# Mixture of experts by dispatch: each row through its two experts only, in place of every row through all eight

## The reference

```python
scores = xf @ gate_w.T                       # 8 experts
ew, ei = jax.lax.top_k(scores, 2)
ew = jax.nn.softmax(ew, axis=-1)
x1 = jax.nn.silu(jnp.einsum('td,ehd->teh', xf, w_gate))      # 128 hidden features per expert
x3 = jnp.einsum('td,ehd->teh', xf, w_up)
expert_out = jnp.einsum('teh,edh->ted', x1 * x3, w_down)
comb = jnp.einsum('ta,tae->te', ew, jax.nn.one_hot(ei, 8))
routed = jnp.einsum('te,ted->td', comb, expert_out)
shared = jax.nn.silu(xf @ sh_gate.T) * (xf @ sh_up.T) @ sh_down.T    # 256 hidden features
return routed + jax.nn.sigmoid(xf @ se_gate_w.T) * shared
```

## Time and profile before

| | us |
|---|---|
| median of 3 runs | 524.58 (524.57 to 527.5) |
| span of the profiled execution, first to last instruction | 524.4 |
| TensorE busy | 485.8 (93%), 3744 matmuls |
| VectorE busy | 383.4 (73%) |
| ScalarE busy | 217.7 (42%) |
| GpSimd busy | 155.0 (30%) |
| mean granted clock of TensorE, as a share of 2.4 GHz | 0.978 |

### The profile page before, as it was taken

One profiled execution on the slowest core, in us unless ns is written; L12 is line 12 of the kernel. 1 busy time (PEld: TensorE's weight loads), 2 busy tenths in 40 slices (PEclk: granted clock), 3 DMA queues, 4 the chain that ended last, 5 costly groups with the idle time before them and its releaser, 6 DMA issues. The chain is left out here.

```text
span 524.4 us, 11913 instructions
## 1 busy us (share of the span) xinstructions
PE 485.8 (93%) x3744; PEld 426.8 (81%) x3744; DVE 383.4 (73%) x1159; ACT 217.7 (42%) x501; POOL 155.0 (30%) x287
## 2 busy tenths in 40 slices
PE   3789999998999999999999999998899889699996
PEld 2567777776888888888888888887888878699995
DVE  5578777777777777777777776788788698666542
ACT  4444555542333333333333335553555444454540
POOL 3434444432111111111111121246455465632100
PEclk9999999999999999999999999998999799899999
DMA  8522222111000000000000000000000000000111
GB/s 279 166 57 62 58 58 58 38 41 45 16 17 16 15 15 15 15 15 15 15 15 15 16 11 11 21 22 22 12 19 20 10 1 2 0 22 22 40 40 42
DMA packets 15088, 18.06 MB, mean 34 GB/s; under 512 B 2001, under 2 KB 14546, under 8 KB 15058
## 3 DMA queue, kind: packets, MB, share of 16 engines
q1 hardware_dynamic: 15058, 17.69, 11.3%
HBM read 15.59 MB, written 2.10 MB: 34 GB/s over the span
## 5 line engine op out<-in xcount | busy, mean ns | idle before, releaser
L251 PE MATMUL PS<-wfh,arena_r 128*128 128x256 f32 (+2 forms) x352 | 121.3, 345 | 1.4 <-DVE arena_r L855 1.4
L252 PE MATMUL PS<-wfl,arena_r 128*128 128x256 f32 (+2 forms) x352 | 116.1, 330 | 0.0
L253 PE MATMUL PS<-wfh,arena_r 128*128 128x256 f32 (+2 forms) x352 | 116.1, 330 | 0.0
L276 POOL TENSOR_TENSOR ve<-mv,eps 128x1 f32<-128x1 f32 x64 | 12.8, 201 | 221.3 <-DVE mv L270 221.0
L251 PEld LDWEIGHTS PS<-wfh,arena_r 128*128 128x128 f32 x352 | 66.6, 189 | 10.1 <-DVE arena_r L855 4.8
L253 PEld LDWEIGHTS PS<-wfh,arena_r 128*128 128x128 f32 x352 | 66.6, 189 | 7.2
L252 PEld LDWEIGHTS PS<-wfl,arena_r 128*128 128x128 f32 x352 | 66.6, 189 | 4.9
L592 ACT ACTIVATE arena_r<-PS 128x512 fp32r<-128x512 f32 (+1 forms) x48 | 25.1, 526 | 62.2 <-PE PS L1187 62.2
L597 ACT ACTIVATE arena_f<-PS 128x512 f32<-128x512 f32 (+1 forms) x48 | 25.3, 527 | 53.0 <-PE PS L253 52.8
L286 DVE TENSOR_SCALAR arena_f<-x,mv,rstd 128x256 f32 (+1 forms) x48 | 37.0, 771 | 13.7 <-POOL rstd L279 13.3
L874 DVE SCALAR_TENSOR_TENSOR arena_f<-arena_f,tiny,PS 128x128 f32<-128x128 f32 x144 | 43.2, 356 | 0.6
(11 more groups left out here) (137 smaller groups left out, 1245.2 us busy)
## 6 DMA issues: line engine op xcount, KB each, us to landing
ctx_raw<-in_ctxT SPq DMA_DIRECT2D x32, 128.0 KB, 2.1
raw<-in_w_ffn SPq DMA_DIRECT2D x16, 241.0 KB, 2.6
raw<-in_w_l SPq DMA_DIRECT2D x16, 192.0 KB, 2.4
out<-arena_f SPq DMA_DIRECT2D x8, 256.0 KB, 2.2
x<-in_x SPq DMA_DIRECT2D x1, 1792.0 KB, 9.9
raw<-in_w_l SPq DMA_DIRECT2D x2, 512.0 KB, 5.0
rows<-in_rows SPq DMA_DIRECT2D x1, 640.0 KB, 6.1
x<-in_x SPq DMA_DIRECT2D x1, 256.0 KB, 2.8
```

Source lines behind the costliest of these rows:

```text
L251: nc.tensor.matmul(out_ap, lh, rh, start=first, stop=False)
L252: nc.tensor.matmul(out_ap, lh, rl, start=False, stop=False)
L253: return nc.tensor.matmul(out_ap, ll, rh, start=False, stop=last)
```

## The change

The router goes into stage 0, and the experts run after it on rows sorted by expert.

- **Stage 0** (`each_slot`: all slots written out, no loop; so too on VectorE and GpSimd in stage 2): in slot `s` tile `s - 3`, whose `x` is complete, is normalised (`route_stats` on VectorE; `route_rstd`, three small operations on GpSimd; `route_norm` on ScalarE), transposed (`route_T`) and split (`route_hi`, `route_lo`) into `xT2h`, `xT2l`, which hold all 2048 tokens by feature in the space of the layer-1 weights. `route`, in slot `s` for tile `s - 4`, makes the scores; VectorE's `route_top` takes the maximum and its index. The last tiles' steps lie in stage 1.
- **Shared expert**: four groups of 512 tokens, two slices of 128 hidden features each, feature-major, so without transposes of the hidden features: `shared_in` (six matmuls of 512, for gate and for up), tanh, two VectorE passes, high and low half, and `shared_out` per tile (six matmuls of 256). `add_shared` adds it to `x` with the sigmoid gate as factor.
- **Places**: `choose` marks each token's two experts; two small plain float32 products (`count_members`, `rank_members`) give each token its rank within its expert; `places` makes its row number, expert `e` having a region of 2176 rows in the DRAM tensor `xs_rows`.
- **Scatter**: `keep_rows` (ScalarE) writes all normalised tiles to `xs`; GpSimd issues two indirect DMAs per tile, 32 in all, each of 128 rows of 1 KB. Block tails are zeroed by SyncE (9 DMAs). `block_table` and `result_places` compute, on VectorE, which expert and rows each of the 40 blocks has and where each result will lie.
- **Blocks**: 40 blocks of 128 rows, in 20 pairs. SyncE reads two row numbers into registers and loads two blocks (128 KB each), four pairs ahead; TensorE transposes them (`block_T`), reads one register word per pair that gives the weight columns, and does `block_in` (per block six matmuls of 256: gate and up of one expert), `block_hT` and `block_down` (three matmuls of 256 per block). ScalarE and VectorE do the halves and the silu. SyncE stores each pair (256 KB) to `ys_rows`. The layer-1 weights are loaded and split beside the blocks.
- **Gather**: after the last store GpSimd gathers for each tile the two result rows of each token (two indirect DMAs), tiles 0 to 2 ahead of stage 2, tile `s + 3` in slot `s` of it; VectorE's `combine` adds them to `x` with their weights (two passes) ahead of the normalisation.

The diff, cut to its core:

```diff
+REGION = TOKENS + P
+BLOCKS, TAIL = 40, 8
+BPAIRS = BLOCKS // 2
...
+            sp.wait_ge(R["tails"], 2)
+            for e in range(EXPERTS):
+                row = sp.value_load(tail_i[0:1, e:e + 1], min_val=0, max_val=XROWS - P)
+                load(xs_d[bass.ds(row, P), :], zeros, tails_zeroed)
+            sp.wait_ge(R["rows"], 1)
...
+            sp.wait_ge(tails_zeroed, 16 * (EXPERTS + 1))
+            sp.wait_ge(rows_scattered, 16 * 2 * TILES)
+            for j in range(4):
+                load_block(j)
+            for j in range(BPAIRS):
+                if j + 4 < BPAIRS:
+                    load_block(j + 4)
+                if j < TILES:
+                    load_w(1, j, j % 2)
+                if j >= 1:
+                    store_block(j - 1)
+            store_block(BPAIRS - 1)
...
+            pool.wait_ge(R["place"], 4)
+            for t in range(TILES):
+                pool.wait_ge(S1["xs"], t + 1)
+                for k in range(2):
+                    nc.gpsimd.indirect_dma_start(
+                        out=xs_d, out_offset=bass.IndirectOffsetOnAxis(posi[:, k, t:t + 1], 0), in_=xs[:, t, :],
+                        in_offset=None).then_inc(rows_scattered, 16)
...
+            def gather(t):
+                if t >= 2:
+                    pool.wait_ge(x_done[1], t - 1)
+                for k in range(2):
+                    nc.gpsimd.indirect_dma_start(
+                        out=gy[:, t % 2, k, :], out_offset=None, in_=ys_d,
+                        in_offset=bass.IndirectOffsetOnAxis(posy[:, k, t:t + 1], 0)).then_inc(y_row_in[t % 2], 16)
+            pool.wait_ge(w_lo, 2 * TILES)
+            pool.wait_ge(R["first"], 6)
+            for r in range(2):
+                pool.wait_ge(y_stored[r], 16 * BPAIRS // 2)
+            for t in range(2):
+                gather(t)
+            for t in range(2):
+                ln_rstd_step(pool, 2, t, t)
+            gather(2)
+            ln_rstd_step(pool, 2, 2, 0)
...
+            for t in range(2):
+                combine(t)
+                ln_stats_step(dve, 2, t, t)
+                ln_aggr_step(dve, 2, t, t)
+            for t in range(2):
+                ln_norm_step(dve, 2, t, t, xn)
+            combine(2)
+            ln_stats_step(dve, 2, 2, 0)
+            ln_aggr_step(dve, 2, 2, 0)
+            for t in range(2):
+                xT_lo_step(dve, 2, t, t, X_T)
+            ln_norm_step(dve, 2, 2, 0, xn)
...
+            for j in range(BPAIRS + 1):
+                if j < BPAIRS:
+                    word = pe.value_load(word_i[0:1, j:j + 1], min_val=0, max_val=(1 << 22) - 1)
+                    gate_at = [pe.snap((word >> 4) & 0x780), pe.snap(word & 0x780)]
+                    down_at[j] = [pe.snap((word >> 11) & 0x700), pe.snap((word >> 7) & 0x700)]
+                    block_in(j, 0, gate_at[0])
+                if j >= 1:
+                    block_hT(j - 1)
+                if j < BPAIRS:
+                    block_in(j, 1, gate_at[1])
+                if j + 2 < BPAIRS:
+                    block_T(j + 2)
+                if j >= 1:
+                    block_down(j - 1, down_at.pop(j - 1))
...
+            pe.wait_ge(w_lo, 2 * TILES)
+            pair_keys(0)
+            for t in range(2):
+                transpose_x(pe, 2, t, t, X_T)
+            pair_queries(0)
```

More of the change, by code:

```diff
@@ L25 @@
 ACT = mybir.ActivationFunctionType
+AXIS = mybir.AxisListType
 P = 128
@@ L109, in slots, with each_slot @@
         body(Slot(s, s % 2, count))
+def each_slot(first, last, body):
+    for s in range(first, last + 1):
+        body(Slot(s, s % 2, TILES))
 def after(eng, sem, t, back=0, base=0, per=1, extra=0):
@@ L373, in build @@
             "o_psum")}
+        R = {n: sem("route_" + n) for n in (
+            "setup", "below", "weights_hi", "weights", "moments", "shift", "xn", "T", "hi", "lo", "psum", "scores", "top",
+            "gap", "gap_e", "mix", "member", "count_psum", "counts", "place", "table", "rows", "words", "tails", "first")}
         S1 = {n: sem("s1_" + n) for n in (
-            "router_psum", "scores", "top", "index", "gap", "gap_exp", "denom", "weights", "w2", "indexf", "pick1",
-            "pick2", "comb", "g_psum", "u_psum", "tanh", "a", "h", "hT_psum", "hT_hi", "hT_lo", "down")}
+            "g_psum", "u_psum", "tanh", "a", "h", "h_hi", "h_lo", "o_psum", "xs")}
+        E = {n: sem("e_" + n) for n in (
+            "T", "x_hi", "x_lo", "gu", "tanh", "a", "h", "hT", "h_hi", "h_lo", "y", "y_out")}
+        x_shared = sem("x_shared")
         S2 = {n: sem("s2_" + n) for n in (
@@ L991, in slot2 @@
                 here, before, leaving, ahead = s.tile(0), s.tile(-1), s.tile(-2), normalised_in(s)
+                if ahead and s.tile(2):
+                    combine(ahead[0])
                 if ahead:
```

819 lines of the change are left out of this document (577 added, 242 removed).

## The result

The changed kernel takes 573.85 us (median of 4 runs, 572.38 to 579.96) against 524.58 before: a ratio of 1.094 (95% interval 1.088 to 1.101), slower where 505 had been forecast. The span of its profiled execution is 571.2, so 46.8 us more than before.

A forecast was written before the change was run, and what follows sets the result against it. TensorE was taken to bound stage 0 and the dense experts, no single engine stage 2. 524.4 + 13.6 (stage 0) - 56 (first shared product to stage 2's queries) + 19 (stage 2) + 4 (clock) = 505 us; range 472 to 540.

The forecast's parts named there:

- Step 1: Stage 0: the router adds 1.0 us a tile on TensorE, +13 over 13 tiles, plus 0.6 before the first shared product.
- Step 2: Shared expert, 512 tokens at a time: the engines are through 42 us after the first shared product (T0').
- Step 3: Scatter: row numbers 16 us after the first shared product (T0'), 32 issues 38.4, then 7.6 to the first expert product.
- X: Price of one indirect DMA issue on GpSimd, taken as 1.2 us; the forecast's range was 0.8 to 1.6.
- Step 4: Expert blocks: 40 blocks in 20 pairs at 3.3 us a pair, 66 us (54 to 90).
- rival (d): Expert blocks run at 4.5 us a pair, by landing times or register reads: +24, 529 in all; chance 0.07.
- Step 5: From blocks to stage 2's queries (Tq'): last output 3.2 us, then 16 with the queries waiting for the third gather.
- Step 6: Stage 2 with gathers: 1.2 us more a tile (0.85 for VectorE's passes, 0.35 more), +19 (0 to +40).
- step 7: TensorE's clock at 1.2 instead of 2.4 GHz: 2 us after each of two stands, +4 (0 to +15).
- (b): Scatter and gathers: the list of indirect DMAs sets both ends; at X = 2.5, 573 us in all; chance 0.16.
- (a): Scatter and gathers: indirect DMA issues are cheap, X = 0.45, 477 us in all; chance 0.20.
- (c): Stage 2: VectorE and GpSimd block each other, a tile costs 10 instead of 7.6, +38, 524 in all; chance 0.07.

The follow-up runs named there:

- the variant of the late transpose: Changed kernel with router statistics one slot earlier, and the router's transpose behind the gate product, its eviction behind the gate's tanh: 539.20 us (ratio 1.022).
- the variant with early statistics: Changed kernel with the router's row statistics taken by VectorE one slot earlier, right behind the addition completing the tile: 552.05 us (ratio 1.052).
- section 6: Row numbers of tiles 0 to 7 made in stage 0, against reordered router, single weight offset, earlier query halves, 2560 descriptor bytes: 530.75 us (ratio 1.007).

## Why the prediction was wrong, point by point

By spans 571.2 against 505.0, 66.2 off: stage 0 +39.0, T0' to Tq' +33.9, the rest -6.8.

**Step 1, the router in stage 0: the step that failed.** The sum of TensorE's work was right (7.5 a tile once the chain is gone). What failed is the sentence "TensorE is the limit, so the work is not hidden: 13 x 1.0": it priced the added instructions and not the wait that came with them. The bound had been named, "a stall of an in-order engine at every tile", +26, and was dismissed without following who must be done before whom: statistics, three GpSimd steps, normalisation, transpose, all inside one slot. That stall, with the clock of 0.84 that it drew after it (1.00 in the same window once it was gone), made +52.7 in place of +13.6, twice the bound that was given. The experiments give back 31.0 of the 39.0. Of the other 8, two waits of 1.84 and 2.67 us are seen in the last two slots (at 133.79 and 138.72 in the variant of the late transpose), which have no gate or query products to hide the chain; the rest was not followed up.

**Step 2, shared expert at T0' + 42:** too short by some 7 us even where nothing stood still (TensorE through at +48.6 in the variant with early statistics), and by 32 here: VectorE's last addition ended at +74, beside the standing still, which no row of before had shown.

**Step 3, scatter.** Numbers at +16: 16.2. X = 1.2: 1.27. Scatter 38.4: 44.4, of which 3.6 are the two pauses of 2.11, beyond the usual gap of 0.30, which no step had; with 2560 bytes for descriptors there was one, of 2.16. The 7.6 to the first product: 17.0, since "The engines' 42 is covered by this" was false here (in the two other profiles of this kernel the first block came 6.4 sooner behind the last issue). For 128 rows an issue took 0.96 on GpSimd and 1.27 from issue to issue, the same for rows of 64 bytes and of a kilobyte. So in a series of 32 it is the issue on GpSimd that counts (44.4 in all); the landing comes once, within the 5.4 from the last issue's end to the first block where nothing stood still.

**Step 4, blocks at 3.3 a pair:** 4.05, 82 us in place of 66. The mis-sized term is "a register read, which no row prices, with some eight register steps of 0.03, 0.2 to 0.5 together": it measured 0.66 to 0.77 a pair, and there were 21 register steps, not eight, at distances of 0.10 or more, not 0.03. Without the register work the pairs come every 3.4 us, near the forecast's 3.3. That was rival (d)'s mechanism, at two thirds of its price; and "if pairs take over 4" was one of the signs of being wrong that the prediction had named.

**Step 5, results back 19.2:** 21.3 (333.2 to 354.45), by the steps told: the third gather sets the queries.

**Step 6, stage 2 at 8.8 a tile, +19, and step 7, clock +4:** step 7's 1.2 GHz is what the trace of before shows at a granted clock of 0.50 (363 to 367): products of 256 columns start 0.213 apart there, 1.2 columns a ns, and 0.12 apart after 369; its 2.4 is the double, for a clock of 1.00. The two steps are together 23, measured 16.2 (18.4 and 20.1 in the two other profiles). The additions took 0.61 and 0.57 a tile, more than the 0.85 counted; the gathers' 0.35 a tile was not there in the run with half of them.

**The rivals.** (b) gave 573 and the measurement is 573.85; it was still not what happened, for X is 1.27, below its point of decision of 1.6. Its number agrees by chance. (a) is out by X. (c): GpSimd's gathers in stage 2 took 0.997 us beside a busy VectorE and 0.979 in the scatter. So the issues show no blocking between the two. VectorE is stretched beside GpSimd's arithmetic, though: 7 of its 26 additions in that stage took 0.73 to 0.96 in place of 0.48, each of them beside GpSimd's own addition to `x` (L651), while its normalisations beside nothing but a gather's issue took 0.41, as alone.

## What to carry to other kernels

When work is moved into a pipelined slot, write down for each added instruction who must be done first, and check that the whole chain of small steps across engines starts a slot before its end is needed; its price is the wait, which the sum of busy times can't show (35 us in stage 0 here). A table-driven loop has a price on the engine that reads the table (0.66 to 0.77 us a pair here): count its register steps and lay data out so that one offset serves all operands. Issuing an indirect transfer earlier helped here only up to the next thing that the blocks wait for (section 6: first issue 5.0 in place of 16.3 behind T0', first block 65.2 in place of 72.9), so look at the releaser of the first block, not at the last issue.

## What the runs showed of the hardware

- An indirect DMA of 128 rows costs GpSimd 0.96 us and follows the last after 1.27, whether a row has 16 or 256 numbers.
- With 2048 bytes for descriptors GpSimd paused 2.11 us after the 14th and the 28th of 32 such issues, with 2560 once, 2.16 after the 17th.
- While a series of them is in the queue, TensorE, ScalarE and VectorE stood still for up to 20.9, 18.2 and 10.6 us, with "issue" or "remote" at the start of the wait, in all kernels of some groups and in none of others. That their instructions are fetched over the same engines that move the rows was not shown. Whether the longer ring makes it worse (20.9 against 11.8 us, one profile each) is open.
- A word load and the 21 steps that take four offsets out of it cost TensorE 0.66 to 0.77 us a pair, and the row of the product that waits for them names VectorE.
- A VectorE addition of 256 columns took 0.48 us alone and, in 7 of 26 cases, 0.73 to 0.96 beside a 256-column addition of GpSimd; its normalisation took 0.41 beside a gather's issue, as alone.
